# A graph attention kernel whose gathers lose their index bound, with an added row of ones for unused slots

## The reference

```python
q, k, v = (x @ Wq + bq), (x @ Wk + bk), (x @ Wv + bv)      # reshaped to (n, H, C)
attn = jnp.einsum('nhc,mhc->hnm', q, k) / sqrt(C)
...
e = jnp.where(mask[None], 0.0, jnp.exp(neg - m))           # mask: adj == 0
alpha = e / jnp.where(denom == 0.0, 1.0, denom)
out = jnp.einsum('hnm,mhc->hnc', alpha, v)                 # then (n, C * H)
x_r = x @ Ws + bs
beta = sigmoid(concat([out, x_r, out - x_r]) @ Wb)
return layernorm(x + beta * x_r + (1.0 - beta) * out)
```

## Time and profile before

| | |
|---|---|
| median of 3 runs | 2084.48 us (2083.2 to 2085.44) |
| the profiled execution | 2082.6 us, of which the span is 2080.8 us |
| DVE busy | 1392.1 us (67%) |
| POOL busy | 1201.6 us (58%), of it 1064.3 us in 1057 gathers |
| PE matmuls busy | 1188.8 us (57%) |
| ACT busy | 760.3 us (37%) |
| moved by DMA | 431.86 MB, 208 GB/s over the span |
| granted TensorE clock | 0.668 of full speed in the mean |

### The profile page before, as it was taken

How to read it: one execution, slowest core, us unless ns; L and a number is a source line. 1 busy time by engine, 2 the same in 40 slices (tenths; PEclk the granted TensorE clock), 3 DMA queues, 4 the chain that set the end, 5 groups by cost and what they waited for, 6 DMA issues and landing times. The chain is left out here.

```text
span 2080.8 us, 19706 instructions
## 1 busy us (share of the span) xinstructions
PE 1188.8 (57%) x4601; PEld 748.1 (36%) x4601; DVE 1392.1 (67%) x3885; ACT 760.3 (37%) x1290; POOL 1201.6 (58%) x1342
## 2 busy tenths in 40 slices
PE   6334454655455455555456455545544353799998
PEld 5113233332233233233223233222233242256887
DVE  5878888887688678878868877877874566121010
ACT  3243233445246234634454454554411001222313
POOL 2347767776777777777767747747676773000000
PEclk9656667666677667668777767767765565655555
DMA  9757666768677677788688868858522232500000
GB/s 369 275 220 265 217 230 250 261 217 294 249 276 265 232 283 281 262 292 305 219 294 307 294 234 289 304 191 304 198 85 80 83 91 99 183 1 0 0 1 2
DMA packets 127968, 431.86 MB, mean 208 GB/s; under 512 B 29310, under 2 KB 62683, under 8 KB 94827
## 3 DMA queue, kind: packets, MB, share of 16 engines
q1 hardware_dynamic: 63194, 291.25, 37.1%
q0 software_dynamic: 55728, 129.92, 19.5%
q10 hardware_dynamic: 8928, 9.44, 1.3%
HBM read 430.75 MB, written 19.31 MB: 216 GB/s over the span
## 5 line engine op out<-in xcount | busy, mean ns | idle before, releaser
L464 POOL DMA_INDIRECT s_kv<-kv_rows,s_rec_in x1057 | 1064.3, 1007 | 402.3 <-issue 329.8
L494 PE MATMUL s_ps_w<-s_mask,s_bit_w 128*128 128x512 bf16 x1008 | 371.0, 513 | 496.9 <-ACT s_mask L576 496.2
L560 PE MATMUL s_acc<-s_kv,ident 128*128 128x128 f32 x2114 | 368.1, 354 | 257.6 <-DVE s_kv L707 257.6
L576 ACT ACTIVATE s_mask<-s_adj_in 128x2048 bf16<-128x2048 f32 x252 | 477.5, 1896 | 48.6 <-PE s_ps_w L494 29.4
L560 PEld LDWEIGHTS s_acc<-s_kv,ident 128*128 128x128 f32 x2114 | 353.5, 265 | 311.0 <-DVE s_kv L707 309.9
L494 PEld LDWEIGHTS s_ps_w<-s_mask,s_bit_w 128*128 128x128 bf16 x1008 | 101.1, 116 | 728.4 <-ACT s_mask L576 612.1
L684 DVE TENSOR_TENSOR s_prod<-s_kv,s_ps_q 128x1792 f32<-128x1792 f32 (+17 forms) x76 | 152.7, 2009 | 121.4 <-DMA s_kv<-kv_rows,s_rec_in 119.9
L609 ACT ACTIVATE s_ps_q<-s_sc 128x56 f32<-128x56 f32 (+17 forms) x76 | 16.8, 221 | 482.6 <-DVE s_sc L698 482.6
L707 DVE TENSOR_TENSOR s_kv<-s_kv,s_ps_q 128x1792 f32<-128x1792 f32 (+17 forms) x76 | 152.6, 2007 | 29.5 <-ACT s_ps_q L609 25.4
L687 DVE TENSOR_REDUCE s_raw<-s_prod 128x56 f32<-128x1792 f32 (+17 forms) x76 | 152.6, 2007 | 6.0 <-issue 0.4
L1166 DVE CUSTOM_DVE_ANT_0 d_sc<-d_ps_s,d_pen 128x1024 f32<-128x1024 f32 x32 | 39.2, 1225 | 165.9 <-PE d_ps_s L1087 165.9
(11 more groups left out here) (195 smaller groups left out, 1465.9 us busy)
## 6 DMA issues: line engine op xcount, KB each, us to landing
s_adj_in<-in_adj SPq DMA_DIRECT2D x247, 1024.0 KB, 7.2
s_kv<-kv_rows,s_rec_in POOLq DMA_INDIRECT x1057
kv_rows<-s_kv SPq DMA_DIRECT2D x16, 512.0 KB, 9.4
s_rec_in<-node_records SPq DMA_DIRECT2D x62, 106.0 KB, 7.6
s_adj_in<-in_adj ACTq DMA_DIRECT2D x5, 1024.0 KB, 19.8
s_kv<-in_x_cols SPq DMA_DIRECT2D x4, 1024.0 KB, 8.4
d_kT<-in_x_cols SPq DMA_DIRECT2D x1, 4096.0 KB, 12.2
d_adj<-in_adj SPq DMA_DIRECT2D x1, 4096.0 KB, 19.8
```

The source lines that it names most:

```text
L464: nc.gpsimd.indirect_dma_start(out=kv[:, k % RING, s], out_offset=None, in_=kv_dram[:, :], in_offset=bass.IndirectOffsetOnAxis(ap=rec_in_u ...
L494: last = nc.tensor.matmul(w[:], bit_w[:, SLABS - 1 - slab], mask[:, k % 2, s * WORD:(s + 1) * WORD], start=False, stop=(slab == SLABS - 1))
L560: last = nc.tensor.matmul(acc[:, c * D:(c + 1) * D], ident[:], kv[:, k % RING, s, D:2 * D], start=(s == 0), stop=(s == SIZES[k] - 1))
L576: nc.scalar.activation(mask[:, q % 2], adj_in[:, q % ADJ_RING], ACT.Sign, accum_out=edges[:, t, h:h + 1]).then_inc(masked, 1)
```

## The change

`kv_rows` gets one row more, number N, which SP fills with ones early (two DMAs of 128 float32, after POOL's second memset). The gathers of k and v have no `bounds_check` any more, so every slot fetches a row. In the list, an unused place now gets exactly N: L768 is split in two DVE operations with a drain between, a maximum with BASE - 1 (times -1) into `cand`, and the addition. POOL waits for the added row before its first gather. The scatter and the store of finished rows keep their bound. The load of the v rows in the dense pass is cut to N rows.

```diff
-        kv_dram = nc.dram_tensor("kv_rows", (N, 2 * D), F32, kind="Internal").ap()
+        kv_dram = nc.dram_tensor("kv_rows", (N + 1, 2 * D), F32, kind="Internal").ap()
...
             for w in range(2):
                 place_x(w)
+            sp.wait_ge(consts, 2)
+            sp.dma_start(kv_dram[N:N + 1, 0:P], ones[:]).then_inc(pad_stored, 16)
+            sp.dma_start(kv_dram[N:N + 1, P:2 * P], ones[:]).then_inc(pad_stored, 16)
...
+            pool.wait_ge(pad_stored, 16 * 2)
             pool.wait_ge(first_listed, 1)
...
                     nc.gpsimd.indirect_dma_start(
                         out=kv[:, k % RING, s], out_offset=None, in_=kv_dram[:, :],
                         in_offset=bass.IndirectOffsetOnAxis(ap=rec_in_u[:, p % RECS, col:col + 1], axis=0),
-                        bounds_check=last_node, oob_is_err=False).then_inc(gathered[k % RING], 16)
+                        ).then_inc(gathered[k % RING], 16)
...
-                last = nc.vector.tensor_scalar(slot[:, LIST_AT:LIST_AT + m], top[:, 0:m], -1.0, float(BASE + N - 1),
-                                               ALU.mult, ALU.add)
+                nc.vector.tensor_scalar(cand[:, 0:m], top[:, 0:m], float(BASE - 1), -1.0, ALU.max, ALU.mult)
+                dve.drain()
+                last = nc.vector.tensor_scalar(slot[:, LIST_AT:LIST_AT + m], cand[:, 0:m], float(BASE + N - 1), None,
+                                               ALU.add)
...
-            act.dma_start(v_rows[:], kv_dram[:, D:2 * D].rearrange("(b p) c -> p b c", p=P)).then_inc(v_in, 16)
+            act.dma_start(v_rows[:], kv_dram[0:N, D:2 * D].rearrange("(b p) c -> p b c", p=P)).then_inc(v_in, 16)
```

More of the change, by code:

```diff
@@ L274, in sparse_tiles @@
         kv_ready = sem("kv_ready")
+        pad_stored = sem("pad_stored")
         kv_stored = [sem(f"kv_stored{i}") for i in range(STAGES)]
```

## The result

The changed kernel takes **2088.92 us**, the median of 12 runs (2087.26 to 2092.89), against 2084.70 us for the kernel before in 12 runs of the same session (2082.34 to 2088.81): a ratio of 1.0022, with a 95% interval of 1.0013 to 1.0031, or 4.2 us slower. A later set of runs gave 2087.25 against 2084.12 us, 1.0018 [1.0009, 1.0027]. So it is slower by about 0.2%, just at what a measurement can tell; 2093 us had been forecast, +8.6 us.

The account below looks back on a forecast made before the run. POOL's gather pace and DVE's lists were taken to bound the kernel in turns. Gather -2.4, landing +1.6 and list +9.4 gave +8.6 us, so 2093 us; the forecast's own range was 2084 to 2106 us, the stated range 2046 to 2106 us.

Parts of the forecast that it names:

- The gather's term: Gathers on POOL (L464) without the bound: 5 ns less for each of 482, -2.4 us; bounds 20 ns either way.
- POOL's stretches: Seven stretches of the sparse part, 693 us long, where POOL's pace sets the time, with 482 of the 1057 gathers.
- Rival A: L464: the check is a real part of each gather; 0.1 us less gives 2047 us, decision point 23 ns; chance 0.30.
- Rival B: L464 against the other costs: gathers 15 to 30 ns shorter cancel +11.0 us, 2085 us, no change; chance 0.18.
- The landing's term: Gathers reading formerly skipped rows land up to 0.46 us later at seven DVE take-overs: 0 to 3.2, taken +1.6 us.
- DVE's stretches: Seven stretches of the sparse part, 927 us long, where DVE's work sets the time, with 36 of the 63 lists.
- the seven hand-overs: Places in the sparse part where DVE takes over from POOL; only there was a later landing said to cost time.
- Rival C: Added row in kv_dram as hot spot: reads of one address take four times as long, about 2125 us; chance 0.08.
- The sign named for C: Adjacency parts would land in over 9 us instead of 7.2 us, with ACT waiting for them.
- The list's term: L768 on DVE: one operation and drain more, 0.26 us, paid whole in 36 of 63 lists, +9.4 us.
- The store of the added row: Two DMAs of 512 B on SP ahead of the first k and v store: 0 us.
- The estimate of 54 us by the bytes alone: Reading skipped rows: 19.5 MB more at 358 GB/s would cost 54 us; the prediction held the trace against it.

## Why the prediction was right, and where it was not

The time and the side were right: 2093 us forecast, 2088.9 measured, and slower. The reasons were half right, and that the sum came out near was luck: two terms, one eight and one twelve times too small, have opposite signs and nearly cancel.

*The gather's term failed.* The step was "the duration does not answer to how many of the 128 rows are skipped", from which 5 ns were taken and 20 ns as the bound. The observation holds, 1006 ns with and without skipping. The prediction had itself said that a test made for every index would not show there, and then priced it at next to nothing. It is 53 ns. By the prediction's own count this gives 482 x 0.053 = 25.5 us. Measured are 20, as for some 380 gathers. The count of POOL's stretches was thus a fair one, and the size a tenth of what it should have been. The comparison with scatter and store could not bound the test, since all three make it and it costs them different amounts. Rival A, at 30%, had the mechanism; it priced it at 0.1 us a gather, twice what came, and its own decision point, 23 ns, was passed. It still did not win, because the 11 us that it had to beat were 24. Rival B, at 18%, came nearest to the shape of the result: two effects that cancel, 2081 to 2088 us. It failed in the sizes of both, 15 to 30 ns against 53 and 11 us against 24, and had itself called such a meeting chance.

*The landing's term failed.* "It is paid where DVE takes over from POOL, seven times", at 0.46 us, with 3.2 us as the end of the bounds. Measured are 18.9 us. Two things were wrong. The rate of the added reads: 143 us on q0 instead of 61. And the place: late landings also came up inside DVE's stretches, where no wait had been (187 and 218 us), so the seven hand-overs were no bound. With the reads spread, the 4 to 7 us left for the bytes may or may not be within it.

*Rival C was the mechanism, with too small a chance.* With 8% it said four times as long and 2125 us. The reads of one address took 143 us of the queue's time where 61 would be the rate of the other rows, 2.3 times; spread over 128 rows they took 49, so the one address made them 2.9 times as long. The argument against it, a first gather in which a fourth of the partitions may read row 0, failed. That gather needs 1.12 us on POOL in the changed kernel and 1.18 before, which says nothing about its landing. The sign named for C was half there: adjacency parts land after 7.6 us, not over 9, and ACT waits 27.1 us for them instead of 18.9. The harm was mainly to the gathers' own landings; what the 8.2 us of longer waits of ACT cost at the end no run separates. The Trainium skill (DMA: Bandwidth & Descriptors, Latency and other measured facts) has row pitches of several MiB at half the rate, with one memory channel as its guess. The factor measured here, 2.3 or 2.9 for reads of one and the same row, is somewhat larger. Whether the cause is the same, no run here shows.

*The list's term had the right sign and was too large.* 36 of 63 lists at 0.26 us gave 9.4; taken alone the list costs 4.9 us (2.5 to 6.3 by the interval), and replacing it by one operation gives 6 to 8. The price of one is right. From DVE's timeline of the changed kernel:

```profile
1549.68 0.18 DVE L773 TENSOR_SCALAR s_cand<-s_top 128x19 f32<-128x19 f32 x1
1549.93 0.35 DVE L775 TENSOR_SCALAR s_rec<-s_cand 128x19 uint32<-128x19 f32 x1
```

The two start 0.25 us apart. What failed was that the 36 lists in DVE's stretches "are paid whole". The 7.1 us by which DVE's waits for gathers fell do not explain it: the prediction had already taken 27 lists, 7.0 us, as covered by them. DVE's busy time grew by 9.2 us, not by 63 x 0.18 = 11.3, which is a part of the difference; where the rest went stays open.

*The rest.* The forecast 149 MB came exactly (149.48). DVE's busy time rose by 8.1 us, not 11. POOL's waits for spots rose, from 68.6 to 113.9 us, far more than the list explains: step by step they are 74.2 with the longer list, 89.9 when the unused slots are read, and 113.9 without the test. The last gather starts at 1739.75 us, 6.1 us later than before, with 8 forecast. The store of the added row, put at 0, was not quite free. From SP's timeline of the changed kernel, and last the same store before:

```profile
12.96 10.00 SPq L362 DMA_DIRECT2D kv_rows<-ones  x1
...
23.96 11.35 SPq L368 DMA_DIRECT2D kv_rows<-s_kv  x8
...
17.49 17.94 SPq L364 DMA_DIRECT2D kv_rows<-s_kv  x8
```

The first of the row's two DMAs stands 10.00 us on SP, and the first store of k and v rows starts at 23.96 us instead of 17.49. SP has caught up by 35 us, but the first gather starts at 79.97 to 80.88 us in the seven ordinary traces with the row, the changed kernel's at 80.61, against 79.61 before. Whether the row is the cause of these 0.4 to 1.3 us, no run separates; they are part of what the table calls the list. The estimate of 54 us by the bytes alone, from the Trainium skill (DMA: Bandwidth & Descriptors, Where 436 GB/s comes from), is not borne out: all that reading the unused slots costs is 18.9 us, and the bytes are the smaller part of it. Most of them travel beside other work.

## What to carry to other kernels

A test whose cost doesn't vary with what it finds can't be read from a trace in which every instruction makes it: bound it by a run with the test and nothing to skip, not by the likeness of its neighbours. Slots that are read for nothing should not all read one row; here one row for each partition won 12 to 15 us. A new slow transfer is not bounded by the waits that the kernel before shows, because it makes waits where there were none; and a sum that comes out right says little of its terms until each has been run alone.

## What the hardware showed that was not expected

- The bound of an indirect DMA costs POOL 53 ns of 1007 for a gather of 128 rows of 1024 B, whether it skips or not. For a scatter it is 13 to 18 ns of 992 and for a store 6 to 11 ns of 1017, by one trace. Why the three differ is open.
- Some 19,000 reads of one row of 1024 B cost the software queue 143 us on each DMA engine, and the same number over 128 rows 49 us.
- On two occasions and two chips the kernel before took 2403 and 2410 us instead of 2084; one of the chips had it at 2085 another time. The traces of the other kernels from these sessions have the usual busy times on DVE and POOL and long waits for issue. The cause is open. There the kernel with the spread rows, 9 us faster at other times, was 25 to 29 us slower than the kernel before.
